# Second layer of a recurrent two-layer kernel: first key matrices before the small scale operations, first chunk turned in the first step, last chunk without a state update

## The reference

```python
q, k, v = (silu(causal_conv(x @ W.T)) for each)      # 6 heads of 64
q, k = l2norm(q), l2norm(k)
beta = sigmoid(x @ Wb.T); g = -exp(A_log) * softplus(x @ Wa.T + dt_bias)
def step(S, inputs):                                  # once per token
    S = S * exp(g_t)
    u = b_t * (v_t - k_t @ S)
    S = S + outer(k_t, u)
    o_t = (q_t * scale) @ S
    return S, o_t
o = rmsnorm(o) * o_norm_w * silu(x @ Wg.T);  s = o @ Wo.T
x = x + s * silu(ffn(xn))                             # sign weights, relu, 2048 wide
```

## Time and profile before

| | before |
|---|---|
| median of 3 runs | 1397.91 us (1397.85 to 1403.75) |
| the profiled execution, its own time | 1397.27 us |
| its span, first to last instruction | 1395.2 us |
| TensorE busy | 1330.5 us, 95% |
| VectorE busy | 1065.5 us, 76% |
| ScalarE busy | 734.8 us, 53% |
| GpSimd busy | 524.1 us, 38% |
| mean granted TensorE clock | 0.997 |

### The profile page before, as it was taken

The page is one execution under the profiler, slowest core; times in us unless marked ns, Lnnn a source line. Parts: engine busy times, 40 slices in busy tenths (PEclk is TensorE's granted clock), DMA queues, the critical chain, the costliest instruction groups (busy, mean ns, idle before and its releaser), DMA issues. The chain is left out here.

```text
span 1395.2 us, 24351 instructions
## 1 busy us (share of the span) xinstructions
PE 1330.5 (95%) x8972; PEld 652.9 (47%) x8972; DVE 1065.5 (76%) x1870; ACT 734.8 (53%) x1305; POOL 524.1 (38%) x434
## 2 busy tenths in 40 slices
PE   5888999999999999999999999999999999999998
PEld 2332333333333333333345548654585546755485
DVE  7889877787877887788857777597685886768855
ACT  5675666556655666566576423365134552354331
POOL 3599852112201321122215642176221753137331
PEclk9999999999999999999999999999999999999999
DMA  6420000000001000100460230102400013002211
GB/s 234 179 84 3 7 8 4 24 30 16 9 14 41 14 8 16 31 24 1 158 267 31 58 61 32 39 8 62 88 17 31 24 46 80 24 23 56 42 24 46
DMA packets 80469, 68.51 MB, mean 49 GB/s; under 512 B 46080, under 2 KB 67296, under 8 KB 77792
## 3 DMA queue, kind: packets, MB, share of 16 engines
q1 hardware_dynamic: 67936, 65.39, 15.2%
q10 hardware_dynamic: 12416, 1.57, 1.1%
HBM read 44.87 MB, written 17.87 MB: 45 GB/s over the span
## 5 line engine op out<-in xcount | busy, mean ns | idle before, releaser
L621 DVE TENSOR_REDUCE mS<-vpair 128x1 f16<-128x512 f32 x512 | 329.1, 686 | 112.8 <-PE vpair L1125 110.6
L936 ACT ACTIVATE probs<-bank 128x512 f16<-128x512 f32 x512 | 277.3, 595 | 163.4 <-PE bank L1132 163.1
L1179 PE MATMUL bank<-rows,both 128*128 128x512 f16 x1024 | 243.0, 380 | 0.4 <-DVE th L650 0.4
L436 POOL TENSOR_TENSOR h<-th,h 128x512 f16<-128x512 f32 x61 | 71.5, 1172 | 219.1 <-ACT h L907 219.1
L1179 PEld LDWEIGHTS bank<-rows,both 128*128 128x128 f16 x1024 | 91.3, 98 | 121.2 <-issue 15.5
L2156 PE MATMUL bank<-rows,both 128*128 128x512 f16 x512 | 117.2, 379 | 0.0
L1125 PE MATMUL vpair<-qk 32*128 32x512 f16 x512 | 99.9, 385 | 18.1 <-DVE mS L621 7.7
L2172 PE MATMUL bank<-both,hid 128*128 128x512 f16 x512 | 111.2, 379 | 0.0
L2140 PE MATMUL bank<-rows,both 128*128 128x512 f16 (+1 forms) x456 | 104.4, 379 | 0.9 <-PEq L160 0.9
L1132 PE MATMUL bank<-qv,qk 32*128 32x512 f16 x512 | 99.5, 385 | 0.0
L1193 PE MATMUL bank<-dn,h 128*128 128x512 f16 x256 | 98.0, 383 | 0.0
(11 more groups left out here) (334 smaller groups left out, 2671.9 us busy)
## 6 DMA issues: line engine op xcount, KB each, us to landing
h<-in_ug SPq DMA_DIRECT2D x8, 1024.0 KB, 5.3
lt_scratch<-big SPq DMA_DIRECT2D x16, 384.0 KB, 2.8
dn<-in_down SPq DMA_DIRECT2D x2, 2048.0 KB, 11.0
x_scratch<-th SPq DMA_DIRECT2D x16, 256.0 KB, 2.2
res<-x_scratch SPq DMA_DIRECT2D x16, 256.0 KB, 4.8
out_x<-res SPq DMA_DIRECT2D x16, 256.0 KB, 2.0
both<-in_w SPq DMA_DIRECT2D x2, 1548.0 KB, 10.4
t_scratch<-tok SPq DMA_DIRECT2D x16, 192.0 KB, 2.1
```

Source lines behind the costliest of these rows:

```text
L436: pool.tensor_tensor(h16(ft, 1), row32, h16(ft, 0), ALU.subtract).then_inc(S["row_lo"], 1)
L621: v.tensor_reduce(mS[:, u % 2, qt, 32 * j + DH:32 * j + DH + 1], SA[n % 2][:, :], AX.X, ALU.max).then_inc(S["max_done"], 1)
L936: a.activation(probs[:, n % (2 * G), :], SB[n % 2][:, :], ACT.Exp, scale=float(DH) ** -0.5).then_inc(S["p_ready"], 1)
L1179: mm = pe.matmul(GB[n % 2][:, :], w[:, kt, col:col + P], xnb(b, kt), start=r == 0, stop=r == 2 * KT - 1)
```

## The change

Three edits, all in the second layer, made for each of the 4 batches. First, VectorE multiplies the first key matrices (KK 0) before the reciprocal, `e5`, `sn` and `sn5`, not behind them. Second, `turn_kv` for chunk 0 is called right behind X5 in step 0, not behind X6. Third, in step 4 nothing of the state update is made (no SU, no decayed state, no sum, no `Kt`), and accordingly `turn_kv` for chunk 3 transposes only the values. The banks' order and the counts that the semaphores are compared with follow.

```diff
+KV = 2 * TT - 1
...
-            v += rec * [(b, "SU", tt - 1)]
+            v += (rec and inv) * [(b, "SU", tt - 1)]
...
                 v.tensor_scalar(ssq[:, :, 0:LH], bk[:, :, 0:LH], 4e-6, float(HD), ALU.add, ALU.mult).then_inc(S["v_took"], 1)
+                matrices("KK", 0)
                 v.wait_ge(S["v_took"], VI[b, "ss"] + 1)
                 v.reciprocal(rsk, ssq[:, :, LH:]).then_inc(S["small_r"], 1)
...
-                matrices("KK", 0)
                 matrices("KQ", 0)
...
-                        v.wait_ge(S["kv_full"], 2 * w + 1)
-                        v.tensor_tensor(heads(Kt), heads(fbank[0][:, 0:KW]), hb(vec[:, rt, LH:2 * LH], HD), ALU.mult).then_inc(S["kv_took"], 1)
-                        v.wait_ge(S["kv_full"], 2 * w + 2)
+                        k = b * KV + 2 * rt
+                        if inv:
+                            v.wait_ge(S["kv_full"], k + 1)
+                            v.tensor_tensor(heads(Kt), heads(fbank[0][:, 0:KW]), hb(vec[:, rt, LH:2 * LH], HD), ALU.mult).then_inc(S["kv_took"], 1)
+                            k += 1
+                        v.wait_ge(S["kv_full"], k + 1)
...
-                        v.wait_ge(S["gcs_r"], (b + 1) * 2)
-                        v.tensor_tensor(ssS[:, :, :], S_[:, cur, :, :], gcs[:, rt, :].rearrange("p (h c) -> p h c", c=1).to_broadcast([P, MT, HD]),
-                                        ALU.mult).then_inc(S["ssS_r"], 1)
+                        if inv:
+                            v.wait_ge(S["gcs_r"], (b + 1) * 2)
+                            v.tensor_tensor(ssS[:, :, :], S_[:, cur, :, :], gcs[:, rt, :].rearrange("p (h c) -> p h c", c=1).to_broadcast([P, MT, HD]),
+                                            ALU.mult).then_inc(S["ssS_r"], 1)
...
                     def turn_kv():
...
                         for i, base in enumerate((MT, 2 * MT)):
+                            if i == 0 and tt == TT - 1:
+                                continue
                             if tt:
-                                pe.wait_ge(S["kv_took"], 2 * (w - 1) + 3 + i)
+                                pe.wait_ge(S["kv_took"], b * KV + 2 * tt - 1 + i)
                             else:
                                 pe.wait_ge(S["fd_r"], b * TT + 3 + i)
...
                     if inv:
                         product_X5()
+                    if tt == 0:
+                        turn_kv()
...
-                    if rec:
+                    if rec and inv:
                         bk = vfill("SU", rt)
...
+                    if 0 < tt < TT:
+                        turn_kv()
                     if inv:
-                        turn_kv()
                         bk = vfill("Z", tt)
```

## The result

| | before | changed |
|---|---|---|
| median | 1400.98 us (11 runs, 1397.46 to 1404.12) | 1392.30 us (11 runs, 1390.15 to 1399.53) |
| the profiled execution, its own time | 1397.27 us | 1390.15 us |
| its span | 1395.2 us | 1388.4 us |
| its mean granted TensorE clock | 0.997 | 0.994 |

The ratio is 0.9945, with a 95% interval of 0.9929 to 0.996: 7.7 us faster by the ratio, 8.7 us by the two medians, where 10.5 us (a ratio of 0.9925) were forecast. The median of before that I started from, 1397.91 us, came of three runs; more runs put it at 1400.98.

A forecast was written before the change was run, and what follows sets the result against it. TensorE, busy 1330.5 of 1395.2 us, was taken as the bound. 6.4 - 1.1 + 3.6 + 1.6 = 10.5 us off 1397.27 us, plus 0.64 us for the runs' median, gave 1387.4 us, range 1385.5 to 1393.0.

The forecast's parts named there:

- KK 0 first: End of the front: KK 0 before the scales removes TensorE's 1.60 us wait before KQ 0, 6.4 us over four batches.
- VectorE's 0.1 us delay: End of the front: VectorE takes the first half of KQ 0 0.1 us late, which TensorE doesn't notice.
- the inversion's cover: Before X5: first block is in place 2.3 us before TensorE asks, so even an inversion not moving along would hide.
- (c): Rival, chance 0.12: the stage of the matrices gives back 0.9 us per batch, 3.6 us in all; 1391.0 us.
- (d): Rival, chance 0.03: VectorE's convolution 8 and silu 8 slow down beside GpSimd's work; 3.0 us slower, 1400.9 us.
- Turn in step 0: Step 0: transposes behind X5 delay Y5, ScalarE's copies and Z by 0.28 us, a loss of 1.1 us in all.
- The time freed behind X6 becomes a wait for ScalarE: Step 0: with the turn gone from behind X6, TensorE waits there for ScalarE's copies before Z; net loss 0.28 us.
- Last chunk: Steps 3 and 4: dropped transposes save 0.40 us and dropped SU 0.50 us, 0.90 per batch, 3.6 us in all.
- the lower bound: End of the last batch: at least 0.4 us of the saving remains if the norm on GpSimd decides.
- The clock: Batch 0 near 780 us: with TensorE's stand gone, the fall to 1.2 GHz goes too, gaining 1.6 us.
- (a): Rival, chance 0.22: the low stretch of the clock stays or turns up at one other place; 8.9 us gained, 1389.0 us.
- (e): Rival, chance 0.07: waits move and the clock falls at several places, say four; 4.1 us gained, 1393.8 us.

The follow-up runs named there:

- experiment 4: Kernel before with only the last chunk's state update and the turn of its keys left out; ratio 0.9981, period 163.36 us.
- experiment 1: Kernel before, unchanged, timed against itself; ratio 1.0001, period 164.33 us.
- experiment 5: Changed kernel with the turn of chunk 0 back at its old place behind X6; ratio to before 0.9915, period 161.70 us.
- 11: Repeat of experiment 5: changed kernel with the turn of chunk 0 at its old place; ratio to before 0.9911.
- 7: Changed kernel run again without edit; ratio to before 0.9946, periods 161.91, 163.53 and 161.91 us.
- 10: Changed kernel run a third time without edit; ratio to before 0.993, periods 161.91, 165.18 and 161.92 us.
- experiment 9: Changed kernel with chunk 0 turned twice in step 0, behind X5 and again behind X6; ratio to before 0.9922.
- experiment 2: Kernel before with only KK 0 moved ahead of the small scale operations; ratio 0.9949, period 162.67 us.
- experiment 8: Kernel of experiment 5 with output O made before the second last but one projection, in the last batch only; ratio to before 0.990.
- experiment 3: Kernel before with only the turn of chunk 0 moved behind X5 of step 0; ratio 1.0019.

## Why the prediction was right in its parts and too high in its sum

**KK 0 first: right.** 1.60 us per batch were forecast, 1.66 measured, with the rows as told (6.5 of the 6.6 us are the four stands); VectorE's 0.1 us delay and the inversion's cover harmed nothing. Rivals (c) and (d) did not come.

**Turn in step 0: right in sign and path.** 0.28 us forecast, 0.22 measured; Y5 came 0.25 us later, and Z waited for ScalarE. What I had written there as harmless, "The time freed behind X6 becomes a wait for ScalarE", was most likely the costly part, by the clock.

**Last chunk: right.** 0.90 us per batch forecast, 0.96 measured. At the end of the program 0.82 us of it remained (experiment 4), and 0.6 us in the changed kernel, whose early turn costs 0.22 there. The mechanism is the one named with the lower bound: after the change VectorE's first operation of `finish` starts only 0.03 us behind the end of GpSimd's norm, which itself came only 0.1 us earlier than before, counted from X5 of batch 3. More than the bound of 0.4 us remained, since before the change VectorE reached that operation only 0.5 us behind the norm: it had first waited for TensorE's projection.

**The clock: wrong, and the step that failed.** The prediction said: "With the stand gone I expect the fall gone: 1.6 us." At its place this was so: there is no low stretch near 780 us any more. But I took the one stretch that I had seen in one execution as the whole of the clock's effect. I did not ask what the new stand of 0.9 us before Z, which had followed from my own rows, would do to it, nor whether another would come at the end.

How much the clock took back can be worked out. Over 61 executions of before and 22 of the changed kernel the mean spans are 1398.7 and 1391.3 us, 7.4 us apart. The traces give what the edits are worth without the clock: 1.66 us in batch 0, three periods of 2.41 us, and 0.6 us at the end, 9.5 us in all (8.9 forecast). So the clock took back some 2.1 us, give or take 1.1, where I had it give 1.6. Its mean fell from 0.9935 to 0.9918; 1.7 thousandths at the 0.95 us measured in experiment 1 are 1.6 us, most of it. Rivals (a) and (e) named this, with chances of 0.22 and 0.07; the measured loss lies between theirs.

Where it was lost, the traces show in part. Behind the stand before Z, the three traced executions of the changed kernel lost 0, 1.6 and 3.3 us. Under the last transposes and projection they lost 1.6, 2.9 and 1.7 us (against the end of experiment 5, which has no low stretch there, plus the turn's 0.22 us), where the two of before lost nothing.

That the early turn costs clock is shown by undoing it alone (experiments 5 and 11 against 7 and 10: 2.5 us beside the path). That it does so by the stand and not by the transposes' new place is made likely by experiment 9, not shown. And it isn't the only cause: experiment 4 has no early turn, and the clock took back 2.0 us there; experiment 2 has neither the old stand nor the early turn, and didn't get the 1.6 us. The kernel with both other edits and the late turn (5 and 11) has a mean span 11.3 us below that of before, where its path gives 10.4: there the clock gave 0.9 us, give or take 1.7, which neither shows nor excludes the forecast 1.6.

**Still open.** The low stretch under the last projection came in nine of the thirteen traces. All nine have a stand of 1.9 to 2.1 us ahead of it; experiment 8, which has none, has no low stretch there. But the two of before and experiment 5 have the stand too, and no low stretch. It isn't the shortened code that brings it: experiment 3 runs the end of the program with the very instructions of before and has it, and of two executions of one kernel, experiments 5 and 11, one has it. So it can differ from execution to execution; I have no experiment that tells what decides, nor how often before has it. The first layer had one to four low stretches per traced execution in unchanged code, one of them often twice as long.

## What to carry to other kernels

A stand of TensorE that costs nothing on the path may still cost by the clock behind it, so filler work that closes such a gap is worth leaving where it is. When work is moved into a wait, compare its length with the wait (0.8 us of transposes in a wait of 0.5 us lost 0.2 us, 0.5 us of them lost nothing), and look at what opens where it stood. Take the clock's share from many executions, not from the one that was profiled.

## What the runs showed of the hardware

Every low stretch of the second layer within TensorE's work came behind a stand, in a stretch where it was otherwise busy; but not every stand had one behind it. Behind the stand of 0.9 us before Z it came in 3 of 16 cases, behind that of 1.6 us in none of 12, behind that of 1.75 us in 4 of 4, and behind that of 1.9 to 2.1 us at the end in 9 of 12. The stretches lasted 3.4 or 6.8 us, and one of 3.4 us cost 1.6 us. The Trainium skill's page "TensorE: Matmul & The Clock Gate", section "What's actually happening", ties the clock to how busy TensorE has been. The traces agree in that the stretches stand behind stands; they don't tell which stand will be followed by one. The same program's executions differ by up to 9 us of span, with mean clocks from 0.990 to 0.998.

A VectorE operation on 24 columns took 0.12 us when GpSimd was between two operations, and 0.93 us on the same operands at its place before, when it started inside one. The Trainium skill's page "SBUF — State Buffer", section "Who interferes with whom", gives an exclusive lock that VectorE and GpSimd share. By it an operation of this kind (`tensor_scalar`, one input in SBUF) is held only in one of VectorE's two-port modes; no run here shows in which mode it ran. The matrix operations with one operand in PSUM ran beside GpSimd unhindered, 1.00 us for two, as the page says.
